# The bias-fold rows of a mixture-of-experts kernel are loaded to 128 partitions instead of 127

## What is computed

```python
x = x + _L0_xattn_ref(_layernorm(x), ctx_1024, Wg, bg, W1, b1, W2, b2)          # A: 8 experts, top 2, gated by the context
x = x + _L0_ffn_ref(_layernorm(x), Wg, W1, b1, W2, b2, W3, b3)                  # B: 16 experts, grouped top 4, gated (silu) FFN
x = x + _L1_xattn_ref(_layernorm(x), ctx_1024, ctx_1024, Wq, Wk, Wv, bv, Wo, bo)  # C: 16-head attention over 256 tokens
x = x + _L1_ffn_ref(_layernorm(x), ln_gamma, ln_beta, fc1_q, fc1_scales, ...)   # D: quantised FFN 128 -> 512 -> 128
```

```python
h = silu(x2 @ W1[e].T + b1[e]) * (x2 @ W3[e].T + b3[e])
y = y + (h @ W2[e].T + b2[e]) * we[:, None]
```

## Time and profile before

| | us |
|---|---|
| median of 3 executions | 886.69 |
| lowest, highest | 886.65, 890.72 |
| the profiled execution, its own time | 887.16 |
| its span (first to last instruction) | 884.2 |

### The profile page before, as it was taken

One profiled execution on the slowest core, in us unless ns is written; L12 is line 12 of the kernel. 1 busy time (PEld: TensorE's weight loads), 2 busy tenths in 40 slices (PEclk: granted clock), 3 DMA queues, 4 the chain that ended last, 5 costly groups with the idle time before them and its releaser, 6 DMA issues.

```text
span 884.2 us, 17572 instructions
## 1 busy us (share of the span) xinstructions
PE 763.7 (86%) x5374; PEld 584.3 (66%) x5374; DVE 633.5 (72%) x1875; ACT 502.1 (57%) x990; POOL 398.2 (45%) x462
## 2 busy tenths in 40 slices
PE   7489787786998889798879999978999998997897
PEld 5478676675887678687668888844555554554675
DVE  6878533453856958666976788677888887885786
ACT  2755433453775466577546677724565555555796
POOL 5447773006710077751037774046766444455100
PEclk9689977987999999989999999989999999999899
DMA  9294556465411222911213432034455446441011
GB/s 325 89 336 147 187 175 205 166 194 172 125 59 48 79 71 65 359 52 27 68 48 90 124 85 56 24 106 120 134 144 145 119 117 177 110 125 49 13 37 48
DMA packets 96368, 106.54 MB, mean 120 GB/s; under 512 B 12604, under 2 KB 70348, under 8 KB 94999
## 3 DMA queue, kind: packets, MB, share of 16 engines
q1 hardware_dynamic: 76856, 78.04, 28.2%
q0 software_dynamic: 8608, 18.22, 8.1%
q10 hardware_dynamic: 10816, 9.16, 3.4%
HBM read 69.19 MB, written 36.18 MB: 119 GB/s over the span
## 4 chain that ended last, share of the span: by engine, by line
PE 52%; DVE 19%; POOL 9%; issue 8%; ACT 4%; ACTq 3%; DMA 3%; SPq 2%; DVEq 0%; POOLq 0%
PE y_ps L1937 4%; PE y_ps L2067 3%; ACTq L1650 3%; PE y_ps L2166 3%; PE hid_ps L2052 3%; POOL yg L657 2%; POOL xr L648 2%; PE hid_ps L2142 2%; PE hid_ps L2154 2%; PE hid_ps L1925 2%; PE hid_ps L2143 2%; PE tr_ps L2222 2%; DVE hl L1147 2%; PE hid_ps L2036 2%; PE y_ps L1939 1%
## 5 line engine op out<-in xcount | busy, mean ns | idle before, releaser
L648 POOL DMA_INDIRECT xr<-b_tokens,idx_sb x70 | 67.5, 964 | 121.8 <-DVE idx_sb L909 100.6
L1147 DVE TENSOR_TENSOR hl<-hid_ps,hh 128x512 fp32r<-128x512 f32 x78 | 53.7, 689 | 87.0 <-ACT hh L1577 86.5
L657 POOL DMA_INDIRECT yg<-a_rows,idx_a x64 | 61.2, 957 | 79.5 <-DMA a_rows<-yo 56.2
L1937 PE MATMUL y_ps<-region,hh 128*128 x312 | 88.3, 360 | 8.9 <-DVE hl L1147 8.4
L1334 DVE TENSOR_REDUCE negmax<-hid_ps 128x4 f32<-128x512 f32 x128 | 85.8, 683 | 7.3 <-PE hid_ps L2143 6.9
L679 POOL DMA_INDIRECT yg<-b_rows,idx_b x64 | 62.3, 973 | 37.9 <-issue 35.5
L1571 ACT ACTIVATE zb<-hid_ps 128x512 f32<-128x512 f32 x78 | 46.5, 596 | 53.9 <-PE hid_ps L1917 42.9
L2143 PE MATMUL hid_ps<-region 128*128 128x512 f32 x128 | 75.9, 594 | 0.0
L2067 PE MATMUL y_ps<-region,hh 128*128 x280 | 74.8, 344 | 0.1
L1937 PEld LDWEIGHTS y_ps<-region,hh 128*128 128x128 f32 x312 | 62.5, 200 | 16.8 <-issue 16.3
L1925 PE MATMUL hid_ps<-ident,zb 128*128 128x128 f32 x312 | 51.7, 292 | 25.1 <-ACT zb L1571 25.1
(11 more groups left out here) (359 smaller groups left out, 2302.6 us busy)
## 6 DMA issues: line engine op xcount, KB each, us to landing
region<-k_strips SPq DMA_DIRECT2D x128, 64.0 KB
region<-k_strips SPq DMA_DIRECT2D x32, 256.0 KB, 3.0
region<-hl SPq DMA_DIRECT2D x128, 64.0 KB
k_strips<-k_halves SPq DMA_DIRECT2D x24, 256.0 KB, 4.3
region<-nought SPq DMA_DIRECT2D x6, 1024.0 KB
a_rows<-yo SPq DMA_DIRECT2D x20, 256.0 KB
b_rows<-yo SPq DMA_DIRECT2D x18, 256.0 KB
staged<-a_w_in SPq DMA_DIRECT2D x16, 256.0 KB, 5.7
```

The lines of the kernel that those rows point to most:

```text
L648: g.indirect_dma_start(xr[:, q % 3, j * RB:j * RB + w], None, src, bass.IndirectOffsetOnAxis(ap=rows.bitcast(U32), axis=0)).then_inc(x_til ...
L657: g.indirect_dma_start(yg[:, b % 2, k, j * P:(j + 1) * P], None, ys[h], bass.IndirectOffsetOnAxis(ap=idx[:, h, k, t:t + 1].bitcast(U32), a ...
L1147: v.tensor_tensor(hl[:, n % 2, :], hid_ps[2 + n % 2][:], hh[:, n % 2, :].bitcast(F32), ALU.subtract).then_inc(a_hl, 1)
L1937: t.matmul(y[:, c0:c0 + 2 * P], hh[:, n % 2, cs], w2a[:, bass.ds(e * (2 * FA) + c * 2 * P, 2 * P)], start=c == 0, stop=False)
```

## The change

The destination of the row copies gets the full 128 partitions of `rt`, and the source pattern repeats the row 128 times instead of 127. The subtraction still reads the first 127. Nothing else moves: the eight loads keep their place, their semaphore and its increment.

```diff
-        def last_row(k):
-            return rt[0:P - 1, raw_slot(k) * BT:(raw_slot(k) + 1) * BT]
+        def row_copies(k):
+            return rt[:, raw_slot(k) * BT:(raw_slot(k) + 1) * BT]
...
-                        v.tensor_tensor(rows, rows, last_row(k), ALU.subtract).then_inc(b_folded, 1)
+                        v.tensor_tensor(rows, rows, row_copies(k)[0:P - 1], ALU.subtract).then_inc(b_folded, 1)
...
-                        a.dma_start(last_row(k), bass.AP(row.tensor, row.offset, [[0, P - 1], [1, BT]])).then_inc(in_raw[raw_slot(k)], 16)
+                        a.dma_start(row_copies(k), bass.AP(row.tensor, row.offset, [[0, P], [1, BT]])).then_inc(in_raw[raw_slot(k)], 16)
```

## The result

The changed kernel takes 848.4 us (847.75 to 848.55, 4 runs) where the kernel before takes 888.71 (886.65 to 892.41, 4 runs): a ratio of 0.9541, 95% interval 0.9502 to 0.9579. The forecast was 847.0 in 841 to 860. The profiled execution took 848.27 us, its span is 846.5, 37.7 less than before, and the mean granted clock is 0.957 instead of 0.942.

What follows compares the result with a forecast made beforehand. ScalarE's block loads, held at issue while one DMA engine drains the 127-row load, stall TensorE; stretches 44.15 us less waits of 1.0, 1.2 and 2.3 take 39.65 off 887.16; with the runs' median 0.47 lower, 847.0 us, range 841 to 860.

Steps and rivals of the forecast that it cites:

- The cause: ScalarE's block-load issues, held up to 10.02 us while one DMA engine drains the 254 KB row load to 127 partitions at 26 GB/s.
- The stretches: Four-step stretches, steps 18 to 46: each stalled one falls to the nearest unstalled one with the same matmuls, 44.15 us saved.
- the waits of 1.0 and 1.2 us: Deductions: 1.0 for second-half tokens and the V store behind them (0 to 4), 1.2 for V stores elsewhere (0 to 6).
- what is late next: Lists that don't get faster: SyncE's tokens and V store 1.0 us, other V stores 1.2, GpSimd's gathers 2.3.
- The gathers' term: GpSimd's 16 gathers of first-half results land at 221.8, VectorE needs them at 219.5: 2.3 us wait, ends 0 and 5.
- A second stall: Rival: any load under way in ScalarE's queue still holds the block's issue 2 to 4 us; 859 to 871 us, chance 0.15.
- Nothing spreads: Rival: the split goes by the one-row source, so 128 rows stay on one engine; 887 us, no change, chance 0.05.
- The slower case: Rival: spread rows delay SyncE's V store to 17 us landings, VectorE waits at each V copy; about +8, 895 us, chance 0.02.

## Why the prediction was right

**The cause** held as put. The trace of the kernel before had the three signs (the held issue, the 26 GB/s tail, the drop of the clock), and the experiments confirm the links: one engine for 127, more for 128, 126, 122 and 112; the hold gone with half the bytes; the hold on the queue that issues the row load. The rule of the Trainium skill, page "DMA: Bandwidth & Descriptors", section "Why a DMA increments its semaphore by 16 and not by 1", agrees with all counts tried: 1, 2, 14, 16, 15 and 16 engines for 127, 122, 126, 112, 15 and 128 rows.

**The stretches**: 44.15 us forecast before the waits of 1.0 and 1.2 us, 41.95 with them, 42.70 measured. Five of seven came within 0.8 us of the value taken for them. Steps 34 to 38 took 14.09 for 12.31, with the V store's wait priced under "what is late next"; steps 42 to 46 took 8.87 for 10.11. The stretch that I took as the measure of these has VectorE's combine in it (busy 9.33 us there, 5.65 here); that this is the reason was not tried.

**What is late next**: of the terms of 1.0 and 1.2 us, 1.78 and 0.9 came. The form differed: the scatters freed SyncE at 147.58, not 144.6, yet the transposition L1900 at 152.41 did not wait for its tokens; the V store did the damage, at 143.44, ahead of SyncE's wait; behind that wait a V copy lost only 0.70. The gathers' term was the one mis-sized: 2.3 us taken, ends 0 and 5, and steps 46 to 54 lost 4.26. I priced the landing of block 1's gathers, for which nothing waited; block 0's made VectorE wait 1.75. And I left out what stands behind block 2's on GpSimd, the power L611, with ScalarE's in-order list behind it.

**The sentence that failed** is that after 230 us no list holds time against the gain. Steps 50 to 54, which started at 229.84 before, took 12.82 us for 11.30, behind the power in GpSimd's list. Steps 66 to 77 lost another 1.97 us (32.82 for 30.85); there it is not a list that holds the time but TensorE, busy 2.04 us longer with the same matmuls at a clock of 0.90 for 0.98. Whether the change put it there is open: the kernel before takes 32.75 us there on the slower chips, and the one with the loads on SyncE 30.66.

**How much was luck.** The forecast took 39.65 us off the profiled execution, and 38.89 came (887.16 to 848.27). The gathers' term and steps 54 to 77 cost 1.96 and 2.02 us more than forecast. Against them stand 3.2 us that the sum did not foresee: 0.75 in the stretches, the 0.82 ahead of step 18, 0.46 behind step 77, and 1.19 outside the span (which shrank by 37.70, not 38.89). So the mechanism was right and the total within 1.4 us of the forecast of 847.0, but part of that closeness is errors that cancel.

**The rivals.** A second stall is out: ten issues at 0.33 to 0.35. Nothing spreads is out. The slower case had its mechanism, two V copies waiting 2.1 us in all, far from the 6.5 us in each of seven stretches that it needed. With the loads moved to SyncE, a V store landed only 10.21 us after its issue, and two V copies waited 4.5 us in all.

## What to carry to other kernels

A DMA issue of microseconds in a compute engine's queue was here a symptom of the DMA that the same queue issued before it: look at that one's partition count, and let the count have a large divisor of at most 16 (128 has 16, 127 only 1), even at the cost of a row that nobody reads, or split it (112 and 15 did as well). Price what a removed stall gives by the nearest unstalled stretch with the same matmuls, not by the length of the stall, since the clock comes with it (8.41 us for 7.31 held). Then read every in-order list that was idle during the stall: GpSimd's gathers, free before, took back about 4 of 43 us.

## What the runs showed of the hardware

The hold sits at the issuing queue, not at the busy engine: ScalarE's loads that need that engine pass in 0.33 us while SyncE, whose long load fills it, is held for about 8. It ends long before the load does, with 86 to 95 rows of its queue still to move in the first profile. How many engines a load uses can be counted in the packets of its queue: 128, 124, 140, 158 and 144 for 127, 122, 126, 112 with 15, and 128 rows. And the gain depends on what else stops the engines: the same edit is worth 4.6% where the kernel takes 887 us and 1.7% (0.6 to 0.9% for its relatives) on chips where it takes 1052 to 1058. There the single engine drains in pauses that are there anyway: at four of the block's issues its backlog was 0 to 70 rows, and none of these was held.
